# Four consecutive rows of x per partition, and transposes that read adj with a step of four elements

## What is computed

```python
bw  = sign(weight)
ba  = maximum(sign(x), 0)          # 1 where x > 0, else 0
xw  = ba @ bw.T                    # 8192 x 256, small whole numbers
g   = relu(adj @ xw)
out = layernorm(x + g, axis=-1)    # eps 1e-5, no scale, no bias
```

## Time and profile before

| | us |
|---|---|
| median of 3 runs | 995.71 (995.62 to 995.8) |
| the profiled execution, its own time | 995.31 |
| its span, first to last instruction | 993.5 |

### The profile page before, as it was taken

One profiled execution on the slowest core, in us unless ns is written; L12 is line 12 of the kernel. 1 busy time (PEld: TensorE's weight loads), 2 busy tenths in 40 slices (PEclk: granted clock), 3 DMA queues, 4 the chain that ended last, 5 costly groups with the idle time before them and its releaser, 6 DMA issues.

```text
span 993.5 us, 12241 instructions
## 1 busy us (share of the span) xinstructions
PE 971.5 (98%) x4484; PEld 802.0 (81%) x4484; DVE 844.5 (85%) x874; ACT 613.2 (62%) x655; POOL 842.0 (85%) x361
## 2 busy tenths in 40 slices
PE   5999999999999999999999999999999999999996
PEld 3788888888888888888888888888888888888885
DVE  4868998989888898988989898898988889898893
ACT  3777675665656566565665656566565666656562
POOL 2666998998889889898998889899888988989893
PEclk9999999999999999999999999999999999999999
DMA  9999999999999999999999999999999999999961
GB/s 281 348 337 332 325 308 334 271 315 287 330 300 289 317 286 319 291 304 311 285 311 295 325 291 296 304 299 314 293 319 297 295 290 316 314 277 329 296 194 40
DMA packets 298459, 294.67 MB, mean 297 GB/s; under 512 B 9376, under 2 KB 298400, under 8 KB 298400
## 3 DMA queue, kind: packets, MB, share of 16 engines
q1 hardware_dynamic: 157792, 155.47, 57.3%
q10 hardware_dynamic: 140608, 138.43, 49.5%
HBM read 285.47 MB, written 8.39 MB: 296 GB/s over the span
## 4 chain that ended last, share of the span: by engine, by line
PE 95%; DMA 3%; SPq 0%; DVE 0%; ACT 0%; POOL 0%; issue 0%; ACTq 0%
PE ps L501 93%; DMA x_sb<-in_x_dram 1%; PE ps L526 1%; DMA raw<-in_adj_dram 1%; PE ps L486 1%; PE ps L476 0%; POOL lo L249 0%; SPq L172 0%; DVE stats L381 0%; SPq L165 0%; DVE rows L377 0%; ACT hi L269 0%; ACT relu L278 0%; ACT rows L286 0%; DVE mv L384 0%
## 5 line engine op out<-in xcount | busy, mean ns | idle before, releaser
L249 POOL TENSOR_TENSOR lo<-turned,hi 128x1024 fp32r<-128x1024 f32 x352 | 840.9, 2411 | 134.7 <-ACT hi L269 130.6
L501 PE MATMUL ps<-hi,xw 128*128 128x512 f32 x2048 | 801.5, 391 | 3.7 <-POOL lo L249 1.9
L501 PE MATMUL ps<-lo,xw 128*128 128x512 f32 x2048 | 798.1, 390 | 0.0
L269 ACT ACTIVATE hi<-turned 128x1024 fp32r<-128x1024 f32 x352 | 373.3, 1061 | 257.1 <-PE ps L501 175.2
L501 PEld LDWEIGHTS ps<-hi,xw 128*128 128x128 f32 x2048 | 385.0, 188 | 84.5 <-ACT xw L262 3.7
L501 PEld LDWEIGHTS ps<-lo,xw 128*128 128x128 f32 x2048 | 385.1, 188 | 79.1
L369 DVE STREAM_TRANSPOSE turned<-raw 128x1024 f32<-128x1024 f32 x352 | 426.3, 1218 | 0.9 <-DMA raw<-in_adj_dram 0.9
L373 DVE TENSOR_TENSOR lo<-ps,hi 128x1024 fp32r<-128x1024 f32 x160 | 195.1, 1220 | 106.0 <-ACT hi L269 105.8
L269 ACT ACTIVATE hi<-ps 128x1024 fp32r<-128x1024 f32 x160 | 163.9, 1024 | 92.5 <-PE ps L501 76.9
L369 DVE STREAM_TRANSPOSE ps<-raw 128x1024 f32<-128x1024 f32 x160 | 194.9, 1218 | 4.1 <-DMA raw<-in_adj_dram 4.1
L286 ACT ACTIVATE rows<-rows,shift,rstd 128x256 f32<-128x256 f32 x62 | 36.2, 586 | 0.0
(11 more groups left out here) (25 smaller groups left out, 42.2 us busy)
## 6 DMA issues: line engine op xcount, KB each, us to landing
raw<-in_adj_dram ACTq DMA_DIRECT2D x254, 512.0 KB, 12.1
raw<-in_adj_dram SPq DMA_DIRECT2D x254, 512.0 KB, 11.0
rows<-in_x_dram SPq DMA_DIRECT2D x16, 512.0 KB, 10.5
out_dram<-rows SPq DMA_DIRECT2D x15, 512.0 KB, 15.8
x_sb<-in_x_dram ACTq DMA_DIRECT2D x14, 256.0 KB, 12.3
x_sb<-in_x_dram SPq DMA_DIRECT2D x14, 256.0 KB, 11.4
raw<-in_adj_dram ACTq DMA_DIRECT2D x4, 256.0 KB, 8.5
raw<-in_adj_dram SPq DMA_DIRECT2D x4, 256.0 KB, 9.0
```

Source lines behind the costliest of these rows:

```text
L249: pool.tensor_tensor(lo[:, n % RING], turned[:, ordinal(n) % TP], hi[:, n % RING].bitcast(f32), ALU.subtract).then_inc(p_los_made, 1)
L269: act.activation(hi[:, n % RING], src, ACT.Copy).then_inc(his_made, 1)
L501: return pe.matmul(acc[b % 2][a], xw[:, step, a * P:(a + 1) * P], part[:, n % RING, k * MB:(k + 1) * MB], start=(step == 0 and part is hi) ...
```

## The change

The view of x is cut differently. Each quadrant's 256 rows of a chunk are now 2 groups (`h`) of 128 rows; in a group, partition j takes the four consecutive rows 4j to 4j+3, one for each of the group's four contraction steps (`b`). Before, it took rows j, j+32, j+64 and so on. For `start_x` this means that a partition's source is one run of 4 rows, 4 KB (two such runs in a piece of 8 steps), where it was 4 or 8 rows of 1 KB that lie 32 KB apart. To match it, `turn` takes for one contraction step every fourth column of adj: the innermost index j of the transpose's source now has a step of four elements, 16 bytes, and k has a step of one, where j had a step of one and k a step of 32. How adj is loaded doesn't change, nor does the number, order, size or output of the transposes.

```diff
-    x_turn = x.rearrange("(c g b j) d -> c g j b d", c=CH, g=G, b=KB)
+    x_turn = x.rearrange("(c g h j b) d -> c g h j b d", c=CH, g=G, h=KB // GK, b=GK)
...
         def start_x(eng, i, quadrants):
+
             first, count = X_PIECES[i]
-            c, k = first // KB, first % KB
+            c, h = first // KB, first % KB // GK
             for g in quadrants:
-                eng.dma_start(x_sb[g * Q:(g + 1) * Q, first:first + count],
-                              x_turn[c, g, :, k:k + count]).then_inc(x_loaded[i], 16)
+                eng.dma_start(x_sb[g * Q:(g + 1) * Q, first:first + count].rearrange("p (h b) d -> p h b d", b=GK),
+                              x_turn[c, g, h:h + count // GK].rearrange("h j b d -> j h b d")).then_inc(x_loaded[i], 16)
...
-                src = raw[:, ch % SLOTS, :].rearrange("p (t k j) -> p k t j", t=NT, j=Q)[:, u * UK:(u + 1) * UK]
+
+                src = raw[:, ch % SLOTS, :].rearrange("p (t h j k) -> p h k t j", t=NT, j=Q, k=GK)
+                src = src[:, u // UPG, u % UPG * UK:(u % UPG + 1) * UK]
                 dve.transpose(dst.rearrange("p (k t j) -> p k t j", k=UK, j=Q), src).then_inc(units_turned, 1)
```

## The result

| | before | after |
|---|---|---|
| median, us (6 runs each, side by side) | 995.64 | 1249.62 |
| range of the runs, us | 995.21 to 995.80 | 1249.25 to 1251.10 |
| span of the profiled execution, us | 993.5 | 1247.7 |

The changed kernel takes 1.2554 times as long, 95% interval 1.2541 to 1.2566. It is 254 us slower, far less than the 412 us that were forecast, and on the side that was forecast.

The account below looks back on a forecast made before the run. TensorE bounds the kernel before, VectorE the changed one: 1383.1 us busy plus 7.7, 10.1 and 5 us idle give a 1406 us span, 1408 us as time. Its own range was 1385 to 1480 us, the whole range 992.5 to 1480.

Parts of the forecast that it names:

- The bound and the threshold: TensorE bounds mid-run; VectorE has 7.1 us slack a block, 0.22 us a transpose, so beyond 1440 ns VectorE bounds.
- one main case to the other: The forecast of a whole second turn, 1408 us, chance 0.43, and the free step, 994.7 us, chance 0.38.
- A second turn for each element: VectorE's transposes: step of four elements adds 1052 ns to each of 512, 1218 to 2270 ns; chance 0.43.
- the upper row: GpSimd's 2411 ns for 1024 elements a partition, taken as upper limit for a transpose, 1193 ns more than now.
- Rival (b): VectorE's transposes: part of a second turn, 1440 to 2200 ns each, time 1000 to about 1370 us; chance 0.15.
- The sum: VectorE's busy time 1383.1 us plus idle 7.7, 10.1 and 5 us: span 1406 us.
- Waits that vanish: VectorE's 105.8 us waiting for hi go and 14.6 us for TensorE's transposes shrink; 5 us put on both.
- The loads: Loads of x ahead of 36 us: longer runs gain 0 to 2.0 us, middle 1.0 us, lost if VectorE bounds.
- rival (a): VectorE's transposes: the step is free, only x's loads count, 994.7 us, between 993.7 and 995.7; chance 0.38.
- rival (c): TensorE's products slow to 0.43 us apart, some 1760 us in all; chance 0.04, shared with a price above GpSimd's.

Follow-up runs that it names:

- the two kernels with a part of the units dear: Kernel before with old loads and the step-of-four transposes in a quarter or three eighths of the units: 997.97 us and 1020.77 us.
- the kernel that carries only its term: Changed kernel's new loads of x with the old transposes of the kernel before: 999.57 us, 1.0043 times before.
- V_UNITS = 4: Changed kernel with VectorE making lo for 4 units of a block in place of 10, GpSimd for 28: 1153.97 us.

## Why the prediction was right in its side and wrong in its size

**The bound and the threshold: right.** The forecast put the decision on 0.22 us of slack for each transpose, and the two kernels with a part of the units dear confirm it: 57.83 us busy against 57.8, 25 us over against 30. The side was right for the reason given. The size was not: the forecast's own range of 1385 to 1480 us missed by 135 us, and 1249.6 us lies inside 992.5 to 1480 only because that range had to reach from one main case to the other.

**A second turn for each element: the term that was mis-sized.** The forecast took 1052 ns more for a transpose, one more VectorE turn of 1.03 ns an element. Measured are 789 ns in the kernel (2007 against 1218) and 734 ns by itself, 0.71 ns an element. An element at such a step takes 1.76 ns in place of 1.04, which is no whole multiple. The forecast's reason against a part of a turn was that no row gave one, and that the value lay near the upper row; that upper row, GpSimd's 2411 ns, was of another engine and no measure of this one. Rival (b), part of a turn, held the transpose in its span of 1440 to 2200 ns. It had a chance of 0.15, and is what happened. The reason that it gave, a clock of the memory that need not be VectorE's, was not tested.

**The sum, redone.** The span forecast was 1406 us and came out at 1247.7. Of these 158 us, 133.0 are the price: 538.6 us were added, and the transposes' durations grew by 405.6 us (1026.8 - 621.2). A further 28.2 us: busy time grew by 377.4 us only, because of other lines. `lo` fell by 4.8 us in sum, the `shift` line by 7.9, and the rest is more overlap between one instruction's end and the next one's start, which the sum of durations doesn't see. VectorE was idle 25.8 us, 3.0 more than the 22.8 forecast. 133.0 + 28.2 - 3.0 = 158.2. The sum of rival (b) has the second of these faults too: with 405.6 us for the transposes it gives 844.5 + 405.6 + 22.8 + 1.8 = 1274.7 us, 25 above the measured time.

**Waits that vanish: right.** The wait for hi ahead of `lo` went from 105.8 us to nothing, the one for TensorE's transposes of x from 14.6 us to 2.8 us. After its last transpose the kernel took 15.1 us (1232.6 to 1247.7), 14.6 were forecast.

**The loads: wrong in sign.** I put them between 0 and 2.0 us of gain and took the middle; they cost 4.0 us by themselves. No row had a run of 4 KB, so no row excluded a loss either, and the bound from 0 upward was not earned: it should have reached to both sides. Its 4.7 MB are also too many: the earlier trace rows count the loads issued by 36 us, not those landed, and the last of them start at 31.8 us with some 12 us to landing. It made little difference to the whole, but it bears on rival (a): even with a free step the change would have been 0.4% slower, not the same. That rival's 0.38 was put on a time of 994.7 us, and the kernel that carries only its term took 999.6.

**TensorE's slower pace, rival (c): in stretches, and without a price.** The prediction named products 0.43 us apart in mid-run as its sign, and they are there. The granted clock fell to 0.50, the 1.2 GHz level, for 3.4 us at a time, once at 34 us and six times between 447 and 827 us. TensorE worked with gaps there (it was busy 4.97 of the 7.60 us ahead of the stretch below). A stretch of the changed kernel, columns as in the earlier trace rows, then TensorE in it:

```profile
597.60:601.00 3.40, 3.40 (x9) 2.67 (x9) 3.40 (x3) 1.37 (x2) 2.40 (x1) 0.50 1.12 217
```

```profile
599.39 0.63 PE L504 MATMUL ps<-lo,xw 128*128 128x512 f32 x1
599.82 0.63 PE L504 MATMUL ps<-hi,xw 128*128 128x512 f32 x1
```

VectorE is busy in all 3.40 us of it. Over the span the clock was 0.988, and the products for hi took 413 ns in the mean against 391. So the argument against (c), that TensorE with gaps had kept the quicker pace from 20.8 to 36 us, does not hold for the whole run; what held is that short stretches hide beneath VectorE.

**Steps and runs against what was cited.** VectorE at steps of 1, 2, 3, 4 and 8 elements takes 1246, 1245, 1531, 1980 and 2006 ns. The Trainium skill ("SBUF — State Buffer", section "SBUF: two separate sides") says that a line of 16 bytes wants at least two hits: this the rows bear out, to the point that 12 bytes, with 1.33 hits a line, lie between. The same note of the Trainium skill has "how far you can stride for free depends on dtype: 4 fp32", which is not so here: a step of 2 fp32 is free, and one of 4 costs the full price. By an estimate from the overhead that the Trainium skill gives ("DMA: Bandwidth & Descriptors", section "Why small descriptors are slow (HBM only)") 4 KB would be 6% quicker than 1 KB; x alone took 32.7 us with 4 KB and 27.9 us with 1 KB, and the measurement decides.

## What to carry to other kernels

Ask of each engine on a hot path how many elements it takes from 16 bytes: with float32 a step of two was free on VectorE and cost ScalarE 68 ns for 1024 elements, and a step of four or more cost 0.7 ns an element on VectorE and 0.9 on ScalarE, whatever its size. Before a layout is changed for the sake of transfers, see whether the transfers are on the chain at all: here 36 of 995 us were, against 512 instructions that paid for it. An engine at 85% has little slack in which to hide a price, and spending nearly the last of it showed here first as spread between runs.

## What the runs showed of the hardware that I had not expected

- Runs of 4 and 8 KB are slower than those of 1 and 2: 8.4 MB into quadrants of 32 partitions took 27.9 us in runs of 1 KB, 27.2 in 2 KB, 32.7 in 4 KB and 37.9 in 8 KB, with no engine computing.
- With the rows of the stationary operand 264 elements apart in place of 256, and the tiles behind it moved, each product of 512 columns took 232 ns in place of 227, 20 us over the kernel. Which of the two does it is open.
- A tiny VectorE instruction with two SBUF inputs (`shift`, 4 elements a partition) takes 686 ns before the change, 160 ns after it, and 724 and 759 ns in the kernels with a quarter and three eighths. The traces show it waiting for the GpSimd subtraction that is under way. In the kernel before, each of the 15 starts within a subtraction and ends 15 to 25 ns after it does; in the changed kernel none of the 15 starts within one. GpSimd's share of busy time alone does not tell: with V_UNITS = 4 it is 93%, and `shift` takes 267 ns, since all 15 start in the last 0.4 us of a subtraction. The rows of before and of after:

```profile
L392 DVE SCALAR_TENSOR_TENSOR shift<-mv,rstd 128x4 f32<-128x4 f32 x15 | 10.3, 686 | 0.0
```

```profile
L395 DVE SCALAR_TENSOR_TENSOR shift<-mv,rstd 128x4 f32<-128x4 f32 x15 | 2.4, 160 | 0.0
```

One of them in the kernel before, and the GpSimd instruction that it starts in (start us, us; it ends at 602.67 us, `shift` at 602.70):

```profile
602.00 0.70 DVE L392 SCALAR_TENSOR_TENSOR shift<-mv,rstd 128x4 f32<-128x4 f32 x1
```

```profile
600.27 2.40 POOL L249 TENSOR_TENSOR lo<-turned,hi 128x1024 fp32r<-128x1024 f32 x1
```
